# Softmax left unscaled until after the values' product, scores by 32-row blocks, sum stores later and a new order on every engine

## The reference

```
q = x Wq + bq; k = x Wk + bk; v = x Wv + bv     # per token: q is 32 (d) x 32 heads, k and v 32 (d) x 8 groups, repeated 4 times
scores[d, e] = sum over heads of q[d, h] k[e, h] / sqrt(32)   # per token: a 32 x 32 matrix
o[d, h] = sum over e of softmax_e(scores)[d, e] v[e, h]
x = ln(x + o)
x = ln(x + fake_quant(x) @ fake_quant(ctx))      # 1024 x 1024 context per sequence
r = sum of the two largest of x gate_w
y = relu(x up_w)^2 down_w + r (x fc1_w) expert_w fc2_w
x = ln(x + (ln(y) * gamma + beta))
```

## Time and profile before

| | |
|---|---|
| median of 3 runs | 663.96 us (660.21 to 665.48) |
| profiled execution | 662.39 us, span 660.5 us |
| granted clock, mean | 0.982 |
| busy: PE, PE's weight load, DVE, ACT, POOL | 604.3, 489.1, 405.1, 306.3, 145.6 us |
| share of the span in the two matmul groups of the feed-forward on the chain | L1582 27%, L1550 27% |
| end of the attention block on PE, first matmul of the feed-forward block | 223.2, 224.5 us |

### The profile page before, as it was taken

One profiled execution on the slowest core, in us unless ns is written; L12 is line 12 of the kernel. 1 busy time (PEld: TensorE's weight loads), 2 busy tenths in 40 slices (PEclk: granted clock), 3 DMA queues, 4 the chain that ended last, 5 costly groups with the idle time before them and its releaser, 6 DMA issues.

```text
span 660.5 us, 7906 instructions
## 1 busy us (share of the span) xinstructions
PE 604.3 (91%) x2960; PEld 489.1 (74%) x2960; DVE 405.1 (61%) x538; ACT 306.3 (46%) x400; POOL 145.6 (22%) x178
## 2 busy tenths in 40 slices
PE   1688999999999899899899999998999999999992
PEld 0576888776775678588788888886888888888881
DVE  5647899999985164344323351235874555759876
ACT  4356578798487263232423433003343433323625
POOL 3414466756463023222300000000000000011000
PEclk9989899999999899899999999999999999999996
DMA  9655655567264458848988756401333335079913
GB/s 338 249 155 143 199 143 186 156 184 239 59 196 180 153 224 305 323 168 303 368 307 295 246 192 192 159 1 61 108 99 99 97 103 193 38 256 317 272 48 127
DMA packets 82103, 123.51 MB, mean 187 GB/s; under 512 B 23825, under 2 KB 50705, under 8 KB 82065
## 3 DMA queue, kind: packets, MB, share of 16 engines
q1 hardware_dynamic: 74592, 95.21, 43.6%
q0 software_dynamic: 5168, 19.40, 8.8%
q10 hardware_dynamic: 2304, 8.39, 3.7%
HBM read 83.13 MB, written 35.65 MB: 180 GB/s over the span
## 4 chain that ended last, share of the span: by engine, by line
PE 55%; DVE 5%; DMA 2%; ACT 1%; issue 1%; SPq 0%; DVEq 0%; ACTq 0%
PE psum L1582 27%; PE psum L1550 27%; DMA u_raw<-in_L_ffn_up_w_dram 2%; ACT u_hi L1624 1%; PE psum L1508 0%; DVE stat_n L1903 0%; PE psum L1516 0%; DVE x1T_lo L1772 0%; PE psum L1517 0%; DVE ffn_hi L1922 0%; DVE ffn_lo L1922 0%; DVE ffn_hi L1911 0%; DVE ffn_lo L1911 0%; DVE u_lo L1776 0%; ACT x1T_hi L1619 0%
## 5 line engine op out<-in xcount | busy, mean ns | idle before, releaser
L1776 DVE TENSOR_TENSOR u_lo<-u_raw,u_hi 128x1024 fp32r<-128x1024 f32 x18 | 23.8, 1322 | 105.1 <-ACT u_hi L1624 105.1
L1550 PE MATMUL psum<-x1T_hi,u_hi 128*128 128x512 f32 x160 | 63.8, 399 | 2.2 <-DVE x1T_lo L1772 2.2
L1550 PE MATMUL psum<-x1T_lo,u_hi 128*128 128x512 f32 x160 | 62.8, 392 | 0.0
L1550 PE MATMUL psum<-x1T_hi,u_lo 128*128 128x512 f32 x160 | 62.6, 391 | 0.0
L1582 PE MATMUL psum<-x1T_hi,x2T_hi 128*128 128x512 f32 x264 | 61.5, 389 | 0.0
L2048 POOL DMA_DIRECT2D x1T_hi<-r_scratch x4 | 2.9, 712 | 264.5 <-PE psum L1582 264.5
L1582 PE MATMUL psum<-x2T_lo,x2T_hi 128*128 128x512 f32 x240 | 56.1, 389 | 3.1 <-DVE x2T_lo L1854 3.1
L1550 PE MATMUL psum<-x2T_hi,u_hi 128*128 128x512 f32 x144 | 56.5, 392 | 2.1 <-DVE u_lo L1776 2.1
L1582 PEld LDWEIGHTS psum<-x1T_hi,x2T_hi 128*128 128x128 f32 x264 | 49.5, 188 | 10.3
L1550 PE MATMUL psum<-x2T_lo,u_hi 128*128 128x512 f32 x144 | 56.1, 390 | 0.0
L1550 PE MATMUL psum<-x2T_hi,u_lo 128*128 128x512 f32 x144 | 56.0, 389 | 0.0
(11 more groups left out here) (256 smaller groups left out, 1326.8 us busy)
## 6 DMA issues: line engine op xcount, KB each, us to landing
d_raw<-in_L_ffn_down_w_dram SPq DMA_DIRECT2D x20, 512.0 KB, 6.4
t_scratch<-d_raw SPq DMA_DIRECT2D x20, 512.0 KB, 4.4
d_raw<-t_scratch SPq DMA_DIRECT2D x20, 512.0 KB, 3.9
c_sb<-in_ctx_dram ACTq DMA_DIRECT2D x16, 512.0 KB, 3.7
u_raw<-in_L_ffn_up_w_dram SPq DMA_DIRECT2D x16, 512.0 KB, 6.5
r_scratch<-f1b SPq DMA_DIRECT2D x10, 512.0 KB, 3.1
r_scratch<-f2b SPq DMA_DIRECT2D x10, 512.0 KB, 3.1
x_sb<-in_x_dram SPq DMA_DIRECT2D x8, 512.0 KB, 4.6
```

The costliest lines, as they stand in the source:

```text
L1550: mm = pe.matmul(acc_b[:, q % 4], s, v, start=(k == 0 and i == 0), stop=(k == KT - 1 and i == 2))
L1776: dve.tensor_tensor(u_lo[:, m % 2], u_raw[:, m % 2], u_hi[:, m % 2].bitcast(F32), ALU.subtract).then_inc(S["u_lo_done"], 1)
```

## The change

Values: `v_bd` gets 36 columns for each of four tokens (four blocks of eight groups and a one, written once by `values_ones`). The exponentials are transposed unscaled. Each product takes the exponentials of one token quarter as the stationary side (128x32) and 36 columns of values as the moving side, so a ninth column holds the sum. `collect` inverts it, multiplies, and transposes. The order of the tokens within 16 is changed at the transposes of x to suit (`by_block`).

Scores: 32 products of 32x32 by 32x128 on the regrouped q itself; `query_diagonal` is gone, and ACT takes two of the four key masks.

`o_n`, `o_tok` and `s_rec` now lie inside the scores buffer `sm`, so the subtraction of the maximum waits for the residual two tiles before, and `load_u` in the attention block waits too. `ungroup` no longer waits for a residual, and `regroup` waits for the scores.

Feed-forward: SP stores three units after the sums' unit, loads b for k >= 2 two units later than before, and puts the load of u first; routing(1) and what follows stand one unit later. All lists of steps in the attention block are in a new order. The parts of them that the prediction speaks of stand in the diff.

```diff
-        s_max, s_sum = sb("s_max", [P, NG * TQ], F32), sb("s_sum", [P, NG * TQ], F32)
-        s_rec = sb("s_rec", [P, 2, NG * TQ], F32)
+        o_n = lambda t: sm[:, t % 2, 0:NG]
+        o_tok = lambda t: sm[:, t % 2, NG:2 * NG]
+        s_rec = lambda t: sm[:, t % 2, 2 * NG]
...
+        by_block = lambda x: x.rearrange("p (n j t) -> p n t j", j=JQ, t=TQ)
+        by_token = lambda x: x.rearrange("p n (j s) -> p (n j) s", j=JQ)
...
             def regroup(t):
                 sp.wait_ge(S["qkv_evac"], t + 1)
                 if t >= 2:
-                    sp.wait_ge(S["q_bd_done"], t - 1)
-                    sp.wait_ge(S["k_bd_done"], t - 1)
+                    sp.wait_ge(S["scores_ready"], t - 1)
...
             def ungroup(t):
                 sp.wait_ge(S["o_done"], t + 1)
-                if t >= 1:
-                    sp.wait_ge(S["pre_done"], t)
...
-                    mm = pe.transpose(tr_ps[:, k], x_sb[:, t % 2, k * P:(k + 1) * P], ident[:])
+                    mm = pe.transpose(by_block(tr_ps[:, k]), x_sb[:, t % 2, k * P:(k + 1) * P], ident[:])
...
             def scores(t):
-                pe.wait_ge(S["q_bd_done"], t + 1)
+                pe.wait_ge(pg_in[t % 2], 16 * NG * (t // 2 + 1))
                 pe.wait_ge(S["k_bd_done"], t + 1)
+                pe.wait_ge(S["k_bd2_done"], t + 1)
...
                 for n in range(NG):
-                    mm = pe.matmul(sc_ps[:, n * TQ:(n + 1) * TQ, :], q_bd[:, t % 2, n], k_bd[:, t % 2, n], start=True, stop=True)
+                    for j in range(JQ):
+                        part = slice(j * HD, (j + 1) * HD)
+                        mm = pe.matmul(sc_ps[part, n * TQ:(n + 1) * TQ, :], pg[part, t % 2, n, 0], k_bd[part, t % 2, n], start=True, stop=True)
...
             def values(t):
...
                 for n in range(NG):
-                    mm = pe.matmul(av_of(t)[:, n], v_bd[:, t % 2, n], smT[:, t % 2, n], start=True, stop=True)
+                    for q in range(TQ):
+                        part = slice(q * HD, (q + 1) * HD)
+                        mm = pe.matmul(av_of(t)[part, n], smT[:, t % 2, n, part], v_bd[:, t % 2, n, q], start=True, stop=True)
...
             transpose_x(0)
+            project(0, 0)
             transpose_x(1)
-            project(0, 0)
             project(0, 1)
-            transpose_x(2)
             project(1, 0)
             project(1, 1)
+            transpose_x(2)
             scores(0)
             project(2, 0)
+            values(0)
             project(2, 1)
-            values(0)
+            transpose_x(3)
             scores(1)
-            transpose_x(3)
             project(3, 0)
+            values(1)
             project(3, 1)
-            values(1)
+            transpose_x(4)
             scores(2)
...
-            def query_diagonal(t):
+            def keys_diagonal(t):
...
-                for j in range(JQ):
-                    ins = act.activation(q_bd[:, t % 2, :, j, :], pg[:, t % 2, :, 0], ACT.Copy, scale=maskj[:, j:j + 1])
+                for q in range(POOL_MASKS, TQ):
+                    ins = act.activation(k_bd[:, t % 2, :, q, :], pg[:, t % 2, :, 1], ACT.Copy, scale=maskt[:, q:q + 1])
...
             def softmax_max(t):
...
                 if t >= 2:
-                    dve.wait_ge(S["smT_done"], t - 1)
+                    dve.wait_ge(S["pre_done"], t - 1)
...
             def collect(t):
                 dve.wait_ge(S["av_ready"], t + 1)
+                if t >= 1:
+                    dve.wait_ge(S["o_done"], t)
...
-                dve.tensor_scalar(o_sb[:, t % 2], av_of(t)[:, :, 0, :], maskt[:, 0:1], None, ALU.mult).then_inc(S["o_part"], 1)
-                for q in range(1, TQ):
-                    dve.wait_ge(S["o_part"], (TQ - 1) * t + q)
-                    ins = dve.scalar_tensor_tensor(out=o_sb[:, t % 2], in0=av_of(t)[:, :, q, :], scalar=maskt[:, q:q + 1],
-                                                   in1=o_sb[:, t % 2], op0=ALU.mult, op1=ALU.add)
+                dve.reciprocal(s_rec(t), by_token(av_of(t))[:, :, GROUPS]).then_inc(S["rec_done"], 1)
+                dve.wait_ge(S["rec_done"], t + 1)
+                dve.tensor_tensor(o_n(t).rearrange("p n (j g) -> p (n j) g", j=JQ), by_token(av_of(t))[:, :, 0:GROUPS],
+                                  s_rec(t).unsqueeze(2).to_broadcast([P, NG * JQ, GROUPS]), ALU.mult).then_inc(S["norm_done"], 1)
+                dve.wait_ge(S["norm_done"], t + 1)
+                dve.transpose(o_sb[:, t % 2], o_n(t)).then_inc(S["o_done"], 1)
...
-            def softmax_sum(t):
-                dve.wait_ge(S["exp_done"], t + 1)
-                dve.tensor_reduce(s_sum[:], sm[:, t % 2], AX.X, ALU.add).then_inc(S["sum_done"], 1)
-                dve.wait_ge(S["sum_done"], t + 1)
-                dve.reciprocal(s_rec[:, t % 2], s_sum[:]).then_inc(S["rec_done"], 1)
...
+            def values_ones():
+                pool.wait_ge(S["wkv_lo_done"], KT)
+                for i in range(2):
+                    for j in range(JQ):
+                        pool.tensor_scalar(v_of(i, j)[:, :, GROUPS], so["ones_bf"][:, 0:NG * TQ], maskj[:, j:j + 1], 1.0, ALU.mult, ALU.mult).then_inc(S["v_ones_done"], 1)
...
-            def softmax_scale(t):
-                pool.wait_ge(S["rec_done"], t + 1)
-                pool.tensor_tensor(sm[:, t % 2], sm[:, t % 2], s_rec[:, t % 2].unsqueeze(2).to_broadcast([P, NG * TQ, HD]),
-                                   ALU.mult).then_inc(S["norm_done"], 1)
...
-            for m in range(2, MU):
-                if m >= 4:
+            for m in range(2, MU + 2):
+                if 4 <= m < MU:
                     load_u(m)
                 for k in range(NP):
-                    if m == sums_at(k):
+                    if m == sums_at(k) + 3:
+                        store_stage(k)
+                        store_t(k)
+                for k in range(NP):
+                    if m == sums_at(k) + (0 if k < 2 else 2):
                         load_b(k)
-                        if k:
-                            store_stage(k - 1)
-                            store_t(k - 1)
-                if m == sums_at(NP - 1) + 1:
-                    store_stage(NP - 1)
-                    store_t(NP - 1)
...
-                if m == 3:
+                if m == 4:
                     routing(1)
-                if m == 4:
+                if m == 5:
                     transpose_logits(1)
-                if m == 6:
+                if m == 7:
                     spread_r(1)
```

More of the change, by code:

```diff
@@ L119, in attention_and_cross @@
         fc2_raw = [x_sb[:, 0], x_sb[:, 1], c_sb[:, 0], c_sb[:, 1]]
[L120 removed]
+        ex_raw = [x[:, 0].rearrange("p n j d -> p (n j d)")[:, h * LAT:(h + 1) * LAT] for x in (wq_own, k_bd) for h in range(2)]
         x2T_hi, x2T_lo = so["x2T_hi"], so["x2T_lo"]
@@ L471, in _ @@
             values(2)
-            transpose_q1(0)
             scores(3)
             transpose_x(5)
+            column_sums(0)
+            project(5, 0)
+            transpose_q1(0)
+            values(3)
+            project(5, 1)
+            transpose_x(6)
             cross(0)
-            project(5, 0)
-            project(5, 1)
-            values(3)
+            scores(4)
             transpose_q1(1)
-            scores(4)
-            transpose_x(6)
-            cross(1)
             project(6, 0)
             project(6, 1)
+            cross(1)
             values(4)
+            scores(5)
             transpose_q1(2)
-            scores(5)
             transpose_x(7)
@@ L1019, in _ @@
-            collect(1)
-            softmax_max(2)
-            xT_lo_out(4)
-            normalise_x1(0)
-            softmax_sum(2)
-            ctx_magic(8)
-            column_term(0)
-            magic(0)
+            normalise_x1(0)
+            xT_lo_out(4)
+            ctx_magic(6)
+            softmax_max(2)
+            magic(0)
+            residual(1)
+            ctx_magic(7)
             softmax_transpose(2)
-            ctx_magic(9)
-            residual(1)
             first_stats(1)
@@ L1042, in _ @@
-            softmax_transpose(3)
+            collect(3)
             residual(2)
             first_stats(2)
+            ctx_magic(11)
             qkv_out(5)
-            values_transpose(4)
-            collect(3)
             normalise_x1(2)
+            xT_lo_out(6)
+            cross_residual(0)
+            magic(2)
             softmax_max(4)
-            xT_lo_out(6)
-            magic(2)
-            softmax_sum(4)
+            residual(3)
             ctx_magic(12)
+            first_stats(3)
@@ L1054, in _ @@
+            values_transpose(5)
+            qkv_out(6)
+            softmax_transpose(4)
+            normalise_x1(3)
             ctx_magic(13)
-            values_transpose(5)
+            collect(4)
+            magic(3)
             cross_residual(1)
-            softmax_transpose(4)
-            residual(3)
-            qkv_out(6)
-            first_stats(3)
-            collect(4)
```

(5 more changed lines are left out.)

427 lines of the change are left out of this document (212 added, 215 removed).

## The result

| | before | changed |
|---|---|---|
| median of the runs | 664.13 us | 639.38 us (4 runs, 636.51 to 643.53) |
| ratio, 95% interval | | 0.964 (0.957 to 0.970) |
| profiled execution, span | 662.39, 660.5 us | 643.53, 641.7 us |
| attention block ends (first transpose of the feed-forward block) | 224.5 us | 209.88 us |
| piece of 576 records begins | 322.94 us | 301.62 us |

The forecast was 653.2 us, 1.6% faster. The direction was right and the range (638 to 680) holds the time, but the size was wrong. The profiled execution is the slowest of the four, so the traces differ by 18.8 us and the medians by 24.7. By the traces, 14.6 us come from the attention block, 6.7 from the first half of the feed-forward block, and 2.8 are lost again in the phases.

A forecast was written before the change was run, and what follows sets the result against it. The prediction took TensorE to set the pace in the attention block, with VectorE nearly full. Waits -7.4 + 2, start -7.3, blocks +9.9 and feed-forward -6.4 gave -9.2 us from 662.4: 653.2 us, range 638 to 680.

The forecast's parts named there:

- I take 37 ns for a record, 2.4 us for each step: Scores and values' products on TensorE: 64 records each, 4.8 us a tile for both steps against 3.56 before.
- if only streaming counts: Values' product: 64 records of 36 columns at 31 ns each, 2.0 us a step.
- Rival A: Scores and values' steps: the blocks overlap fully, 1.8 and 2.0 us, 645 us in all; chance 0.20.
- waits up to the end of attention, and the slow clock behind one: TensorE's waits for collection (3.5 us) and xT_lo (2.4) go, with 1.5 of slow clock: -7.4, 2 taken back.
- start: project(1) at: Start: project(0) no longer waits for tile 1 of x, so project(1) starts at 30.3 us, 7.3 us earlier.
- blocks: Scores and values' products cut into small records: 1.24 us more a tile, 9.9 us over eight tiles on TensorE.
- feed-forward: TensorE's stops at routing (4.3 us) and for u_lo (2.1 us) go: 6.4 us less.
- The 2 us taken back: Allowance in the attention block for about 1 us of waiting at the first values' product and a tighter tail.
- B: Scores and values' steps: issue sets the pace, 56 ns a record, 3.6 us each, 672 us; chance 0.17.
- D: Scores blocks run one after the other: 7.1 us for 2.4, 38 more, 691 us; chance 0.12.
- C: Switches of loaded operand width drain TensorE: 0.17 us each, 32 switches, 5.3 us, 658.5 us; chance 0.06.
- E: Start and feed-forward: waits only move, so gains of 13.7 us do not come, 667 us; chance 0.10.

The follow-up runs named there:

- the repetition: The changed kernel run once more, unaltered, for its spread and a second profile: median 640.16 us, ratio 0.961.
- the early split: Changed kernel with the first low split of x2T on VectorE ahead of the last latent product's collection, not behind it: 634.55 us, ratio 0.956.

## Why the prediction was wrong

The step that failed is "I take 37 ns for a record, 2.4 us for each step". Scores took 1.88 us, 29 ns a record; values 0.70, 11 ns. Against the 1.78 us of each before, that is 8 x (0.10 - 1.08) = -7.8 us where the sum had +9.9, a difference of 17.7. The mistake is in how I bounded it. For the scores I let four blocks run at a time from below; for the values I set 31 ns, "if only streaming counts", as if the array had one stream. But the values' products use a quarter of the columns each, and their neighbours in the inner loop use the other quarters. The low bound should have been 2.0 / 4 = 0.5 us. Rival A (645) was nearest, and it too carried the 2.0. How far the term accounts for the miss can be estimated from the run with the values' loops exchanged, where two thirds of a longer step reached the end: two thirds of 17.7 are 12 us, and 639.4 and 12 make 651, near the forecast. The rows of before could not show this, for no two narrow products on different columns stand next to each other there; only the loop order in the diff told it.

By the other steps, from the trace of the changed kernel:

| step | forecast | measured |
|---|---|---|
| waits up to the end of attention, and the slow clock behind one | -7.4 + 2 | waits from 8.6 to 7.0 us (-1.6), clock in 65:80 from 0.89 to 1.00 (-1.5, as counted in the forecast): -3.1 |
| start: project(1) at | 30.3, -7.3 | 31.33 and 30.95, -6.3 to -6.7; worth 4.0 to 4.6 by experiment |
| blocks | +9.9 | -7.8 |
| feed-forward | -6.4 | -6.7 in the trace, 8.5 by the ratio of its own run |
| slow clock in the phases | none | +2.8 in the profiled run |
| sum | -9.2 | -21.1, and the span fell 18.8 |

*Waits.* The 8.6 us are the 5.9 of the earlier trace rows and 2.7 in smaller ones, the 7.0 all of the list above but x1T_lo's, with 0.6 in rows left out. The waits for the collection went, and of the 2.4 us for xT_lo 0.9 did, since three waits of 0.5 us stand where one stood. The 2 us taken back came as 3.8 us at the transposes of q1 in the profiled run, 1.9 in the repetition. *Start.* Right in kind, and a microsecond short: the second half of project(0) begins only at 24.74, behind the transposes of tile 1, and its twelve pairs of 0.35 us end at 29.0, not at 27.2. Behind it TensorE ran until 34.8 us with 0.64 us a pair, a slow clock that the forecast left as it was. *Feed-forward.* Right. *The sum.* These are readings of one trace, and that they come near its 18.8 us is in part luck, since parts did not add in the experiments.

*Rivals.* B (56 ns a record) and D (blocks in series) did not come in this loop order. D's mechanism is real: exchanging two loops calls it up, 5.9 to 8.5 us a step against the 7.1 given. C: the block scores with a change of the loaded width on either side take as long as the full ones beside the same neighbours, or 0.12 us longer, and the values' step stands 0.20 us above the 0.5 of four at once. By these differences a change costs at most 0.1 us. The Trainium skill (TensorEngine Tiling (Array Packing), Key Properties) says that changing the tiling mode drains the TensorE; if it does here, it costs by these differences less than the 0.17 us I had put on a switch; no run here isolates it. Its other statement there, that different tiles can load and multiply in parallel, the trace bears out with 11 ns a record, and it should have set my lower bound. E (waits only move) fell for the start and the feed-forward. In another place it is what happens: the new values' product in the old orders moved its gain into waits, of VectorE for the residual's transfers and of TensorE for ScalarE.

What the forecast's reasoning missed altogether is that parts did not add. I priced the work gone from VectorE by the waits visible before. The row sum put back costs 6.7 to 8.4 of its 9.7 us, and either half of the change alone is slower than the kernel before.

The attention block of the same code ends at 205.87 us (with the early split, which lies far behind it), 209.21 and 209.88 in three executions. Two rows, from the changed kernel and from its repetition, show most of the difference:

```profile
31.33:34.80 3.47, 3.47 (x11) 2.98 (x12) 1.63 (x10) 2.79 (x3) 0.00 (x0) 0.53 0.38 63
...
148.00:156.00 8.00, 8.00 (x85) 5.75 (x86) 7.93 (x10) 4.40 (x6) 2.96 (x2) 0.80 0.38 115
```

The low clock behind the start costs some 1.6 us in both; the early split's execution had 1.00 there. The first then loses 1.9 us in two waits for xa_out, the repetition 1.6 us by the 0.80 from 148 to 156. So the early split's 3.7 to 5.3 us can hold some chance of this kind. Open is what decides in an execution whether the clock falls.

## What to carry to other kernels

When a product is cut into quarters of the array, price the order of the loop and not the record: neighbours in different quarters overlap, neighbours in the same one run in series. Price work in a chain (scores, softmax, values) by how much slack the order leaves it, not by the waits that stand there now, and test a reorder and a shorter step together before dropping either: here they paid only together. A wait of 3 us on the matmul engine can cost as much again in clock; look at the stretch behind each.

## What the runs showed of the hardware

- Four narrow products run at once if neighbours in the order use different quarters: 64 records of 36 columns in 0.70 us, 64 records of 32 rows by 32 columns over 128 in 1.88 us, with mostly four starts in each 33 and 109 ns. In one quarter at a time: 1.89 us and 5.9 to 8.5 us, with mostly one start in each 33 and 109 ns at full clock.
- The two passes of a single fp32 product, which follow each other in the same quarter, did not stop the others from filling the gaps: 29 ns a record against 92 (5.88 / 64) at the best in one quarter.
- The granted clock fell from 1.00 to 0.50 without any idle time of TensorE, within a scores step that used one quarter at a time; in the changed kernel's middle stretch it was 1.00, and 0.98 in the repetition.
- Behind the same stop of 3.1 us the same 786 records took 178.4, 180.1 or 181.2 us, against 178.2 without the stop.
